# A decoder layer: gates, mixer and feed-forward taken into the same unrolled program as the MLP, in half-steps

## The reference, cut to what matters

```python
# 1. mamba block, then an MLP
x = x + mamba(x)                     # u, in the kernel
a, g = split(rms(x) @ fc1_w.T)       # 256 -> 2 x 1024
x = x + (a * silu(g)) @ fc2_w.T      # 1024 -> 256
# 2. mLSTM mixer, 4 heads of 64; q = layernorm(x), k = v = ctx
ig = [q, k, v] @ igate_w.T + igate_b;  fg = [q, k, v] @ fgate_w.T + fgate_b
cs = cumsum(log_sigmoid(fg))
log_D = cs - cs_shift.T + ig.T,  -inf above the diagonal
m = max(log_D);  C = (q @ k.T / 8) * exp(log_D - m)
h = (C / (max(abs(sum(C)), exp(-m)) + 1e-8)) @ v
x = x + layernorm(h by head) * (1 + out_w)
# 3. feed-forward of width 704, operands rounded to FP4 by blocks of 16
y = q4(layernorm(x));  h = silu(y @ q4(w_gate).T) * (y @ q4(w_up).T)
x = x + q4(h) @ q4(w_down).T
```

## Time and profile before

| | us |
|---|---|
| median of 3 runs | 643.76 |
| lowest, highest | 642.89, 647.67 |
| the profiled execution | 642.77 |
| its span, first to last instruction | 640.8 |

### The profile page before, as it was taken

The page is one execution under the profiler, slowest core; times in us unless marked ns, Lnnn a source line. Parts: engine busy times, 40 slices in busy tenths (PEclk is TensorE's granted clock), DMA queues, the critical chain, the costliest instruction groups (busy, mean ns, idle before and its releaser), DMA issues. The chain is left out here.

```text
span 640.8 us, 9632 instructions
## 1 busy us (share of the span) xinstructions
PE 580.8 (91%) x3055; PEld 471.2 (74%) x3055; DVE 448.5 (70%) x978; ACT 248.9 (39%) x536; POOL 140.8 (22%) x192
## 2 busy tenths in 40 slices
PE   6799996899999988999999999879976699999995
PEld 5576664688888877877888888758864477777774
DVE  5885899698974135342454456457898999999994
ACT  2566765744554322121111110154532444444431
POOL 3110000254442111111011000202766322222200
PEclk9899998999999989998999999599985899999998
DMA  8200000000000500000000000134410000000000
GB/s 289 92 3 0 1 13 5 6 6 6 6 3 2 234 0 0 1 1 16 2 17 17 1 17 16 35 92 121 122 49 2 0 10 16 16 16 16 16 17 25
DMA packets 22527, 20.99 MB, mean 33 GB/s; under 512 B 12120, under 2 KB 20696, under 8 KB 22104
## 3 DMA queue, kind: packets, MB, share of 16 engines
q1 hardware_dynamic: 22008, 20.41, 9.8%
q10 hardware_dynamic: 480, 0.07, 0.1%
HBM read 16.04 MB, written 2.34 MB: 29 GB/s over the span
## 5 line engine op out<-in xcount | busy, mean ns | idle before, releaser
L716 PE MATMUL ps<-xnT,w_fc 128*128 128x256 f32 x512 | 115.7, 387 | 0.0
L716 PEld LDWEIGHTS ps<-xnT,w_fc 128*128 128x128 f32 x512 | 98.7, 194 | 13.6
L1468 PE MATMUL ps<-w_fc,scores 128*128 128x352 f32 x256 | 82.6, 477 | 5.9 <-ACT scores L1534 5.9
L1097 DVE TENSOR_TENSOR xs<-ps,xs 128x512 f32<-128x512 f32 x32 | 22.1, 692 | 76.2 <-ACT xs L915 76.2
L1468 PEld LDWEIGHTS ps<-w_fc,scores 128*128 128x128 f32 x256 | 49.0, 197 | 33.0 <-ACT scores L1534 6.9
L915 ACT ACTIVATE xs<-ps 128x512 f32<-128x512 f32 x32 | 19.1, 597 | 110.2 <-PE ps L716 69.9
L729 PE MATMUL ps<-zs,xs 128*128 128x256 f32 x256 | 56.6, 379 | 0.0
L729 PEld LDWEIGHTS ps<-zs,xs 128*128 128x128 f32 x256 | 48.6, 190 | 6.6
L992 DVE SCALAR_TENSOR_TENSOR fold<-xpad,conv_w,fold 128x256 f32<-128x256 f32 x120 | 50.9, 479 | 0.9
L1486 PE MATMUL ps<-u_res,hT 128*128 128x256 f32 x192 | 45.9, 390 | 3.8 <-DVE scores L1640 2.8
L539 POOL TENSOR_TENSOR bc<-xs,head_c 128x512 f32<-128x512 f32 x16 | 25.5, 1599 | 103.6 <-PE ps L634 77.0
(11 more groups left out here) (259 smaller groups left out, 1168.1 us busy)
## 6 DMA issues: line engine op xcount, KB each, us to landing
xs<-in_ctxT SPq DMA_DIRECT2D x16, 256.0 KB, 3.3
zs<-in_ffn_w SPq DMA_DIRECT2D x1, 2112.0 KB, 9.4
x_res<-in_x SPq DMA_DIRECT2D x8, 256.0 KB, 7.6
w_fc<-in_w_fc SPq DMA_DIRECT2D x1, 2048.0 KB, 10.4
xs<-xnT SPq DMA_DIRECT2D x8, 256.0 KB, 3.4
xs<-in_ctx SPq DMA_DIRECT2D x16, 128.0 KB, 2.6
out<-scores SPq DMA_DIRECT2D x16, 128.0 KB, 1.7
...
```

The source lines that it names most:

```text
L716: last = pe.matmul(bank[half + r][:, i * S:(i + 1) * S], m.w_fc1[:, kk, col:col + P], m.xnT[:, b, kk * S:(kk + 1) * S], start=(kk == 0), s ...
L1097: dve.tensor_tensor(hid[:, p, 2 * pair:2 * pair + 2, :].rearrange("p k t -> p (k t)"), bank[r][:], gate[:, r, :], ALU.mult).then_inc(g["hi ...
L1468: last = pe.matmul(bank[1 + j][:, 0:HALF], xT[:, p, k * P:(k + 1) * P], m.w_gu[:, k, j * HALF:(j + 1) * HALF], start=(k == 0), stop=(k == ...
```

## The change

There is one program, `program`, without a barrier. After step 17 it has slots. The MLP takes 17 slots, two a batch: an even one with one pair of `fc1` and both halves of `fc2` of the batch before, an odd one with three pairs of `fc1`. Four of the mixer's batches stand in slots 12, 13, 14 and 16, four in 20, 22, 24 and 26 (`MIX`; a late batch spreads over four slots). Tile t of the feed-forward starts in slot 14 + t, from the ninth tile on one later (`FWD`); its stages follow with lags 1 (rounding of x), 2 (turn in), 3 (`gate_up`), 4 (`product`, rounding of h), 5 (`down`), 6 (`output`). Slots 17 to 36 are the late ones.

Gates are computed as rows: four matmuls a batch with 48 stationary columns (zeros around the batch's own eight) and 256 tokens moving, accumulated over four batches in one bank. So the gate chain runs twice, on 16 rows of 256 tokens each: in slots 10 and 11, and in 18 and 19 (`CHAIN`), with the logarithms' 13 instructions now on 256 columns of 16 partitions. `turn_weights` (9 groups) stands in slots 7 to 11 on one bank. `gate_up` has three banks of 472 columns, gate and value side by side, as three calls; the hidden vector is turned in two halves through one bank. `quantise` has an eighth in each of slots 2 to 9. PSUM is dealt out anew: `fc1` has two buffers for batches 0 to 5 and one for 6 and 7 (`ring`), since the mixer has banks 3 to 5. `mix_rstds`, `mix_residual`, `tile_rstd`, `mix_variance`, `mix_scale`, `mix_weights` and `mix_normalise` do what `rstds`, `residual`, `tile_rstd`, `variance`, `scale`, `weights` and `normalise` did, with the same instructions and shapes; so do `turned_in`, `norm_in`, `silu_up`, `mix_exps`. The hardware loops and their register semaphores go.

The core of the diff (mostly new lines; the removed programs are left out):

```diff
-        together(gates, mixer_and_ffn)
+        together(program)
...
+    MIX = [12, 13, 14, 16, 20, 22, 24, 26]
+    EARLY = 4
+    FWD = [14 + t + (1 if t >= 2 * EARLY else 0) for t in range(T)]
+    SLOTS = FWD[-1] + 7
+    CHAIN = [10, 18]
+    LF_AT, NM_AT, PARTS_AT = 15, 20, 25
+    mix_at = lambda slot, late=0: MIX.index(slot - late) if slot - late in MIX else -1
+    early_at = lambda slot, late=0: mix_at(slot, late) if mix_at(slot, late) < EARLY else -1
+    late_at = lambda slot, late: mix_at(slot, late) if mix_at(slot, late) >= EARLY else -1
+    started_by = lambda slot: sum(at <= slot for at in FWD)
+    tile_at = lambda slot, late: FWD.index(slot - late) if slot - late in FWD else -1
...
+    ring = lambda n: n % 2 if n < PAIRS * 6 else 0
...
+        def store_max(half):
+            sp.wait_ge(chain_dve[half], PARTS_AT)
+            sp.dma_start(max_dram[half * ROWS:(half + 1) * ROWS], max_parts).then_inc(g["max_stored"], 16)
...
+        for slot in range(SLOTS):
+            j = slot // 2
+            if slot % 2 == 0:
+                on(norm_gate, MLP + j - SCAN - 2)
+                on(norm_sum, MLP + j - SCAN - 4)
+            else:
+                on(q_rstds, j - 1)
+            on(mix_residual, late_at(slot, 3))
+            on(add_mamba, slot)
+            if slot == 1:
+                clear_for_mixer()
+            if slot == 9:
+                clear_for_rest()
+            for late in (0, 1):
+                on(mix_rstds, early_at(slot, 1) if late == 0 else late_at(slot, 2))
+            on(mix_residual, early_at(slot, 1))
+            on(tile_rstd, tile_at(slot, 0), n=T)
...
         def fc1(b, pair):
+            n = PAIRS * b + pair
+            r = ring(n)
             pe.wait_ge(s["xnT_ready"], b + 1)
             pe.wait_ge(s["later_in"], 16 * len(LATER))
             pe.wait_ge(s["seg_read"], 2 * T)
-            pe.wait_ge(s["y_sum"], T - 1 + r)
-            after(pe, g["hid_ready"], n - 1)
-            for half, base in ((0, 0), (2, HM)):
+            pe.wait_ge(s["off_ready"], B)
+            pe.wait_ge(s["y_sum"], T)
+            after(pe, g["hid_ready"], n - 1 if n < PAIRS * 6 else n)
+            for to, base in ((3 * r, 0), (3 * r + 1, HM)):
                 for i in range(2):
                     col = base + (2 * pair + i) * P
                     for kk in range(KD):
-                        last = pe.matmul(bank[half + r][:, i * S:(i + 1) * S], m.w_fc1[:, kk, col:col + P],
+                        last = pe.matmul(bank[to][:, i * S:(i + 1) * S], m.w_fc1[:, kk, col:col + P],
                                          m.xnT[:, b, kk * S:(kk + 1) * S], start=(kk == 0), stop=(kk == KD - 1))
             last.then_inc(g["fc1_ps"], 1)
...
         def gates(b):
+            i, p = b % EARLY, b % 2
             pe.wait_ge(g["qT_ready"], b + 1)
             pe.wait_ge(k_in[p], 16 * (b // 2 + 1))
             pe.wait_ge(s["weights_summed"], 1)
+            pe.wait_ge(s["xnT_ready"], XN_MOVES)
+            after(pe, g["gates_read"], b // EARLY)
+            for k in range(2 * KD):
+                src = m.xnT[:, b, k * S:(k + 1) * S] if k < KD else kT[:, p, k - KD, :]
+                last = pe.matmul(bank[7][0:3 * ROWS, 0:S], m.gate_pad[:, k, 12 - XH * i:12 - XH * i + 3 * ROWS], src,
+                                 start=(i == 0 and k == 0), stop=(i == EARLY - 1 and k == 2 * KD - 1),
+                                 skip_group_check=True)
+            last.then_inc(g["gates_ps"], 1)
...
+        def mix_args(b):
+            pe.wait_ge(r_in[b % 2], 16 * (b // 2 + 1))
+            pe.wait_ge(g["gates_done"], b // EARLY + 1)
+            pe.wait_ge(g["hid_ready"], PAIRS * 6)
+            after(pe, x["h_read"], b)
+            after(pe, x["w_ready"], C * b)
...
+        def gate_up(t, i):
+            pe.wait_ge(f["fxT_ready"], t + 1)
+            pe.wait_ge(g["hid_ready"], PAIRS * B)
+            pe.wait_ge(g["w_saved"], W_GROUPS)
+            if i == 2:
+                pe.wait_ge(g["x1_ready"], T)
+            after(pe, f["h_prod"], t)
+            for k in range(KD):
+                last = pe.matmul(bank[i][:, 0:GU_W], xT[:, t % 2, k * P:(k + 1) * P],
+                                 w_gu[:, k, i * GU_W:(i + 1) * GU_W], start=(k == 0), stop=(k == KD - 1))
+            if i == 2:
+                last.then_inc(f["gu_ps"], 1)
...
+        for slot in range(MLP_SLOTS):
+            j = slot // 2
+            if slot % 2 == 0:
+                on(mix_args, early_at(slot), n=B if slot < 2 * B else 0)
+                on(fc1, j, 0)
+                if slot == 0:
+                    turn(B - 1, 0)
+                    turn(B - 1, 1)
+                    project_out(B - 1, 0)
+                    project_out(B - 1, 1)
+                on(turn_xn, j + 4)
+                on(mix_scores, early_at(slot), n=B if slot < 2 * B else 0)
+                on(fc2, j - 1, 0)
+                on(turn_weights, 2 * (slot - 7), n=W_GROUPS)
+                on(mix_sums, early_at(slot), n=B if slot < 2 * B else 0)
+                on(fc2, j - 1, 1)
+                on(turn_weights, 2 * (slot - 7) + 1, n=W_GROUPS)
+            else:
+                on(mix_args, early_at(slot))
+                on(fc1, j, 1)
+                on(turn_weights, 2 * (slot - 7), n=W_GROUPS)
+                on(mix_scores, early_at(slot))
+                on(fc1, j, 2)
+                on(turn_q, j - 1)
+                on(mix_sums, early_at(slot))
+                on(fc1, j, 3)
+                on(turn_weights, 2 * (slot - 7) + 1, n=W_GROUPS)
+                on(gates, j - 1)
+            if slot == CHAIN[0] + 1:
+                turn_rows(0)
+            if slot == 2 * B:
+                mix_args(EARLY - 1)
+                on(turn_in, tile_at(slot, 2), n=T)
+                mix_scores(EARLY - 1)
+                mix_sums(EARLY - 1)
+        for slot in range(MLP_SLOTS, SLOTS):
+            on(mix_scores, late_at(slot, 1))
+            on(turn_out, tile_at(slot, 5), 0, n=T)
+            on(gate_up, tile_at(slot, 3), 0, n=T)
+            on(turn_out, tile_at(slot, 5), 1, n=T)
+            if slot == MLP_SLOTS:
+                turn_q(B - 1)
+            on(gate_up, tile_at(slot, 3), 1, n=T)
+            on(mix_args, late_at(slot, 0))
+            on(turn_in, tile_at(slot, 2), n=T)
+            if slot == MLP_SLOTS:
+                gates(B - 1)
+            on(gate_up, tile_at(slot, 3), 2, n=T)
+            on(down, tile_at(slot, 5), n=T)
+            on(mix_sums, late_at(slot, 1))
+            if slot == CHAIN[1] + 1:
+                turn_rows(1)
...
+        for slot in range(MLP_SLOTS):
...
+            if slot % 2 == 0:
+                on(silu_gate, j - 1, 3)
+                on(mix_exps, early_at(slot), n=B if slot < 2 * B else 0)
+                on(silu_gate, j, 0)
+                if slot == 0:
+                    for c in range(C):
+                        squares(B - 1, c)
+                        turned_y(B - 1, c)
+                on(squares2, j + 5)
+                on(normed, j + 4)
+                on(turned_weights, 2 * (slot - 7), n=W_GROUPS)
+                if slot == CHAIN[0]:
+                    chain_exp(0)
+                on(turned_weights, 2 * (slot - 7) + 1, n=W_GROUPS)
+                if slot == 2 * B:
+                    lift_x(tile_at(slot, 1))
+                    mix_exps(EARLY - 1)
+                    turned_in(tile_at(slot, 2))
+                on(mix_squares, early_at(slot))
+            else:
+                on(mix_exps, early_at(slot))
+                on(silu_gate, j, 1)
+                on(turned_xn, j + 4)
+                on(turned_weights, 2 * (slot - 7), n=W_GROUPS)
+                on(silu_gate, j, 2)
+                on(turned_q, j - 1)
+                on(turned_weights, 2 * (slot - 7) + 1, n=W_GROUPS)
+                if slot == CHAIN[0] + 1:
+                    chain_last_exp(0)
+                on(mix_squares, early_at(slot))
+                on(lift_x, tile_at(slot, 1), n=T)
+            on(norm_in, tile_at(slot, 0), n=T)
+        for slot in range(MLP_SLOTS, SLOTS):
+            on(turned_out, tile_at(slot, 5), 0, n=T)
+            on(turned_out, tile_at(slot, 5), 1, n=T)
+            if slot == MLP_SLOTS:
+                turned_q(B - 1)
+            on(mix_squares, late_at(slot, 2))
+            on(lift_x, tile_at(slot, 1), n=T)
+            on(lift_h, tile_at(slot, 4), n=T)
+            if slot == CHAIN[1]:
+                chain_exp(1)
+            if slot == CHAIN[1] + 1:
+                chain_last_exp(1)
+            on(turned_in, tile_at(slot, 2), n=T)
+            on(mix_exps, late_at(slot, 0))
+            on(norm_in, tile_at(slot, 0), n=T)
+            on(silu_up, tile_at(slot, 3), n=T)
...
+        def product(t):
+            dve.wait_ge(f["sg_ready"], t + 1)
+            after(dve, f["hT_ps"], 2 * (t - 1))
+            dve.tensor_tensor(pieces3(hf[:, t % 2, 0:3 * GU]), ps[:, 0:3, GU:GU_W], pieces3(sg), ALU.mult)\
+               .then_inc(f["h_prod"], 1)
...
```

(83 more changed lines are left out.)

1072 lines of the change are left out of this document (482 added, 590 removed).

## The result

The changed kernel takes 697.34 us (median of 4 runs, 696.0 to 702.22) against 643.33 for the kernel before in the same runs: 1.0875 times as long, 95% interval 1.0838 to 1.0913. The forecast was 669, with a range up to 684: the sign was right, and the loss is twice the one forecast. The profiled execution took 696.0 for a span of 694.2 (mean granted clock 0.933; before: 640.8 and 0.960).

The account below looks back on a forecast made before the run. TensorE was taken to bound the MLP stage, VectorE with TensorE close behind the forward stage. Slot 10 at 326, then 28, 86, 48 and 179 us gave a span of 667, plus 2.0 around it: 669 us, range 634 to 684.

Parts of the forecast that it names:

- the 6.7 us of gates, turns of q and of weights: By the start of slot 10, TensorE's added work: gates 3.5, a q turn 0.45, six groups of weight turns; 6.7 us onto 322.28.
- I take 326, since two other waits of before have other work in them: Start of slot 10 put at 326 us, crediting two old waits, some 3 us in the first MLP window.
- The chain: Slots 10 and 11: VectorE's logarithms, 13 instructions on 256 columns, take 6.9 us; slot 12 starts 28 us after 326.
- the DMA: Start of slot 12: mix_args(0) was to come at 354 us after a wait on the DMA of the running maxima.
- The 86: Slots 12 to 16: TensorE work of 77 us plus listed waits, with slot 17 starting 86 us after slot 12, at 440.
- The order of events: Slots 17 to 20: first product 17 us into slot 17, then VectorE sets the pace; 48 us, to 488.
- The plain ring: Late slots without mixer: gate_up, down, output, product wait for each other in a loop of 9.4 us; before, 8.3.
- slots 21, 23: Odd mixer slots: mix_sums follows down and mix_normalise stands ahead of product; 14.8 us each.
- Even slots: Slots 20, 22, 24, 26: ScalarE's load, exps, norm_in, load, silu_up, then product: 12.9 us, or 12.3 without norm_in.
- Slots 24 and 25: No gate_up in 25; turn_out(7) waits for the last VectorE step of 25, mix_rstds stands before tile_rstd; 22.6 us.
- the third rival's: Late slots: after gaps TensorE's clock drops to half, 12 to 19 us more, 681 to 688; chance 0.10 with table price.
- Rival 1, the totals: Whole kernel: each slot costs what its fuller engine needs, late slots average under 10 us, 620 us; chance 0.16.

Follow-up runs that it names:

- combo: Changed kernel with output behind tile_stats, product ahead of mix_normalise, second gate chain in slots 17 and 18, silu_gate(7, 3) ahead of norm_in(1): 672.96 us.
- warm_all: warm2 with three more groups of unused transposes in the MLP stage, ahead of turn_q(4), fc2(7) and mix_scores(3): 688.87 us.
- combo_silu: combo with silu_up ahead of mix_exps on ScalarE and mix_scores behind the second gate_up call on TensorE: 684.13 us.
- combo3: combo2 with unused transposes ahead of turn_q(4), mix_scores(3) and gate_up in slot 18, and in slot 28: 660.99 us.
- warm: Changed kernel with unused transposes on TensorE in gaps ahead of gate_up in slots 18, 19, 22, 24, 27 and 28: 695.78 us.
- chain17: Changed kernel with the second half's gate chain a slot earlier, in 17 and 18 in place of 18 and 19: 694.33 us.
- warm2: warm without the filler in slot 27, against the changed kernel: 687.06 us, ratio to before 1.061 to 1.071.
- combo2: combo with output at the head again in slot 25 and norm_in behind silu_up in the mixer slots: 664.51 us.

## Why the forecast missed, by its own steps

Span 694.2 against 667: 27.2 us, in five places.

- **Up to slot 10, 334.8 against 326 (8.8).** The moved work was right: the 6.7 us of gates, turns of q and of weights stand in the timeline one by one. Wrong was the step "I take 326, since two other waits of before have other work in them": no wait vanished, that is 3 us. The other 5.8 come and go with the execution: combo, with the same code up to there, begins its fourth gates at 327.05, 5.9 earlier than the changed kernel. 2.2 of them are there at the start of the MLP stage (202.76 in place of 200.56), 1.9 already behind the last matmuls of the mamba block. In code that both kernels share, behind the same waits of 3.27 and 1.29 us (with transposes between), the four matmuls took 3.49 and 3.25 in this execution; before's were

```profile
103.53 2.75 PE L625 MATMUL ps<-fold,xnT 128*128 128x512 f32 x4
...
116.98 1.88 PE L625 MATMUL ps<-fold,xnT 128*128 128x512 f32 x4
```

- **Slots 10 and 11, 29.8 against 28.** The chain held (reciprocal of 16 x 256 in 1.74, taken 1.7; `turn_q(4)` waits 1.9, taken 1.6); `fc1` behind that wait took 5.04 in place of 3.62. `mix_args(0)` was released by `hidden`, by the profile, and not by the DMA as I had said; in warm_all, combo_silu and combo3 it was the DMA, after 1.2 us.
- **Slots 12 to 17, 94.4 against 86.** The 86 is a slip: the terms of the prediction are 77 of work and 2.4 + 1.6 + 1.0 + 5 + 4 = 14 of waits, 91 together. That is 5 us of the miss, by arithmetic alone; with 91 the forecast would have been 674. The waits came to 10.5: slot 13 had 0.6 and not 2.4, `fc2(7)` 4.0 and not 5, slot 16 3.2 and not 4, slot 15 the 1.6 and 1.1 expected. Behind the waits of 4.0 and of 2.5 for the exps, `fc2` lost 1.8 us, the sums 2.4 and the scores 0.7 to the clock; scores of 2.34 and not 2.1 are another 0.7, gates of 1.86 and not 1.7 another 0.5. So 5 - 3.5 + 4.9 + 1.2 = 7.6 of the 8.4 have a name. Two other executions of the same code (warm, chain17) took 91.4, with the sums at 3.1 in place of 5.4 and the scores at full clock.
- **Slots 17 to 20, 46.1 against 48.** The order of events was right: the first product ends 15.4 us in (17 said), then VectorE is all but full, 28.7 of 29.6 us.
- **Slot 20 to the end, 189.1 against 179.** The plain ring was 9.54 (9.4), slots 21, 23: 14.8, 14.8 (14.8; its terms as written add to 14.65). Even slots had the right chain but 14.7 and 15.2 in place of 12.9 and 12.3: with the clock low, `gate_up` and the arguments end 1.7 to 2.7 us later, and the exps with them, which warm2 gives back in slot 22 (12.5; in slot 20, where its first call ran slow again, it took 15.1). Slots 24 and 25 took 24.6 (22.6), in warm2 22.8. Slot 26 took 13.0 (14.5), 27 13.0 (13.5), 28 13.0 (11.4) and 29 11.2 (9.4), the last two with slow calls; from the first `gate_up` of slot 33 to the end it was 26.1 (24.5).

So the step that failed is the third rival's: "I price it at nothing in the forecast because a gap of 2.47 us is followed by both". The price stood in the text, 12 to 19 us and a time of 681 to 688, and got a chance of 0.10 together with another. In the forecast's own terms the slow matmuls on the path cost 1.9 us ahead of the MLP stage, 1.4 in slot 11, 4.9 in slot 16, and 2.7 and 1.8 in the slots that warm2 repaired: 12.7 us, the largest single term of the 27. Slots 20, 28 and 29, another 5 us over the forecast, had slow calls as well; where their calls run at full clock they take 13.0 and 9.5 (20 and 29 in chain17) and 11.2 (28 in warm2), the forecast's 12.9, 9.4 and 11.4 to 0.2 us. Slots 26 and 27 came 2.0 shorter than forecast and hide part of it. A second count, an estimate, agrees: in slices of 2 us with a granted clock under 0.8, TensorE is busy 45.8 us before and 72.8 after, and half of the difference, some 13 us, is TensorE time lost, part of it in slots 18 and 19, where it cost the kernel nothing. The Trainium skill (TensorE: Matmul & The Clock Gate, HAM oscillation — how this bites in real kernels) describes a loop that pays the slow clock anew behind every wait; the trace agrees for slots 18, 19, 22, 24 and 28, behind waits of 3.2 to 7.2 us. The sum that came out 5 us short and the 3 us of waits credited are the next terms. Even the rival's 681 to 688 lay under the 697 measured: with these 8 us it would have read 689 to 696.

Rival 1, the totals, was wrong where the profile could have said so: the mixer stage of before (427 to 474 us) ran with TensorE busy 45.3 of 47 us, the forward stage with both engines full. Moving one into the MLP stage, full on TensorE, could win only the gate stage and the passage between mixer and forward (474 to 524 us, TensorE busy 35.3 of 50). With the six edits of combo2 the order still needs 664.5; why it stays 21 us over the kernel before was not tested.
